# Three PSUM banks for attention scores and one for turned probability blocks, in place of two and two

## The chip, the cores and the metric

The kernel runs on one core of one Trainium2 chip. The metric is the device time of one execution in microseconds (us), lower is better. Times without a unit below are us too.

## The reference, cut to what matters

Two layers over `x` of shape (2, 512, 256). The first is a state-space layer and a mixture of experts; the change doesn't touch it. The second is causal attention with 32 query heads and 8 key/value heads of 64, gated by a small sign network:

```
q, k, v = h @ Wq.T, h @ Wk.T, h @ Wv.T      # 32, 8 and 8 heads of 64; rope on q and k
logits  = where(causal, q @ k.T / 8, min)
attn    = softmax(logits)
out     = (attn @ v) reshaped to (2, 512, 2048) @ Wo.T
x       = x + out * silu(sign_ffn(layernorm(x)))
```

## The kernel before

The program is written engine by engine: TensorE (PE), ScalarE (ACT), VectorE (DVE), GpSimd (POOL) and SyncE (SP, which issues DMAs) each run a list of their own in order, and meet at semaphores. PSUM is cut by hand into 8 banks of 128 x 512 f32, `bank[0]` to `bank[7]`.

Attention runs over 8 groups `g` (one key/value head each). A group has 4 pairs `i` (2 batches times 2 pairs of query heads, `PAIRS`), and each pair is cut into 5 units `k`, so that a unit fills one bank: `SCORES[k]` says which query blocks of 128 rows, with their causal columns, share it. Units are numbered `u = 5 * q + k` with `q = 4 * g + i`; there are 160. Per unit the work is:

- S: PE makes the scores (2 or 4 matmuls of kT, qT, and one that adds the mask) in the unit's score bank; DVE takes the row maxima (L1074, L1070).
- E: ACT takes exp of the score bank into `prob` (L1334), with row sums by the accumulator read behind each.
- N: DVE takes the reciprocal of the sums (L1079) and POOL scales `prob` (L1532), once per head of a pair.
- T: PE transposes four 128 x 128 blocks of `prob` (L1570) into the unit's turned bank. ACT copies that bank, rounded, into `p_hi` (L1341), and then DVE subtracts `p_hi` from the same bank into `p_lo` (L1083).
- A: PE multiplies the values by `p_lo` and `p_hi` (L1908) into banks 4 and 5. After a head's last unit, O on ACT takes it out (L1353) and R on DVE takes the rest (L1092).

Banks 6 and 7 are for making q for the next group (Q, on DVE rope `r`, L1040 and L1041, then `h`, the copy L1308 on ACT) and for the output projection (W, eight matmuls, L1919 to L1922).

The function `schedule(kind)` sorts all of this by step numbers written by hand, for the first group, the middle ones (1 to 6), the last (7, which makes no q) and the tail. In step n come S and E of unit n, T of unit n - 6 (`LAG`) and A of unit n - 8. Every engine takes its operations of a step in the order of their second numbers. Ten steps (half a group) give this list, with Sik for unit k of pair i; the other half is the same with other pairs:

```
step  PE                ACT                DVE
0     S20 T04 A02 W     T04 E20 O00        S20 N T04 W
1     S21 T10 A03 W     T10 E21 Kh         S21 T10 R00 W
2     S22 T11 A04       T11 E22 Vh O01     S22 T11
3     S23 T12 A10 Q     T12 E23 VO         S23 N T12 R01 Vl
4     S24 T13 A11 Q     T13 E24            S24 T13 r
5     S30 T14 A12       T14 E30 O10        S30 N T14 r
6     S31 T20 A13       T20 E31            S31 T20 R10
7     S32 T21 A14       T21 E32 O11        S32 T21
8     S33 T22 A20       T22 E33 h          S33 N T22 R11
9     S34 T23 A21       T23 E34            S34 T23
```

Before, scores alternate between banks 0 and 1, and turned blocks between banks 2 and 3. So S of unit u waits for the exp of unit u - 2, and T of unit u waits for `p_lo` of unit u - 2. The semaphores `exp_done` and `plo_done` start at 2, so that the waits read:

```
pe.wait_ge(exp_done, u + 1)     # S
pe.wait_ge(plo_done, u + 1)     # T
```

Before attention the values of the first batch (`make_v(t)`, t = 0 to 3, six matmuls each, L1574 to L1576) go through banks 0 and 1. Those of the second batch (t = 4 to 7) are made in the first four steps of group 0, between scores, through banks 2 and 3, and ACT copies each out (L1301).

Of the kernel before, what the change touches and what calls it, by code (L numbers as in the profile page):

```python
# [160 lines left out]
PICKED = 2  # L161
CHUNK_AT = [3 + 11.5 * c for c in range(NT)]
Q_MOVES = 4 * 16 * GQ


def q_moved(b, groups):
# [9 lines left out]
def layered_kernel(nc, x, params, consts, select, rope, w_in, w_out, w_moe, w_moe_tail, w_qkv, w_o, w_sign, out):  # L176
# [4 lines left out]
    with ctx:  # L181
# [501 lines left out]
        def _(dve):  # L683
# [376 lines left out]
            def attend(now, steps):  # L1060
                for late, op, i, k in steps:
# [1 line left out]
                    q = g * PAIRS + i  # L1063
                    u = q * 5 + k
                    if op == "S":
                        bk = bank[(i + k) % 2]
                        dve.wait_ge(score_full, u + 1)
                        segs = SCORES[k]
                        if k == 2:
# [7 lines left out]
                    elif op == "N":  # L1077
                        dve.wait_ge(exp_done, q * 5 + (HEADS_AT[k] + 2))
                        vec.reciprocal(rinv[:, i % 2, k, :], rsum[:, i % 2, k, :]).then_inc(rinv_ready, 1)  # L1079
                    elif op == "T":  # L1080
                        b_ = (i + k) % 4
                        dve.wait_ge(phi_done, u + 1)
                        TT(p_lo[:, b_, :], bank[2 + b_ % 2][:, :], p_hi[:, b_, :].bitcast(F32), ALU.subtract).then_inc(plo_done, 1)  # L1083
                    elif op == "R":
                        b, m = i // 2, i % 2
                        dve.wait_ge(ohi_done, 2 * q + k + 1)
                        if q == 0:
                            dve.wait_ge(o_zero, 1)
                        if k == 1 and m == 0 and q > 0:
                            dve.wait_ge(wo_full, g * (BATCH * KC) + 2 * b + 1)  # L1090
                        to = o_rest1[:, m, :] if k else o_rest0[:, b, m, :]
                        STT(out=to, in0=o_hi[:, b, m, :].bitcast(F32), scalar=minus[:, k:k + 1], in1=bank[4 + k][:, :],  # L1092
                            op0=ALU.mult, op1=ALU.add).then_inc(olo_done, 1)
                    elif op == "W":
                        b, m = i // KC, i % KC
                        cs = slice(b * HALF, (b + 1) * HALF)
                        dve.wait_ge(wo_full, g * (BATCH * KC) + (i + 2))
                        if g == 0:
                            vec.tensor_copy(sT[:, m, cs], bank[6 + m][:, :]).then_inc(w_added[m], 1)
                        else:  # L1100
                            TT(sT[:, m, cs], sT[:, m, cs], bank[6 + m][:, :], ALU.add).then_inc(w_added[m], 1)
                    elif op == "M":
                        cs = slice(k * HALF, (k + 1) * HALF)
                        dve.wait_ge(w_added[i], (KVH - 1) * BATCH + (k + 1))
                        dve.wait_ge(g1_ready, KC * (k + 1))
                        TT(sT[:, i, cs], sT[:, i, cs], g1T[:, i, cs], ALU.mult).then_inc(sg_ready, 1)
                    elif op == "X":
                        dve.wait_ge(back_full, i + 1)
                        xt2 = x_tok[:, 2 * i:2 * i + 2, :]
                        TT(xt2, xt2, bank[i][:, :].rearrange("p (t c) -> p t c", c=C), ALU.add).then_inc(x_ready, 1)  # L1110
                    elif op == "r":
                        if now == 0 and i == 1 and k == 0:
                            dve.wait_ge(q_first, 2)
                        rope_q(now * 2 + i, k)
                    elif op == "qa":
                        dve.wait_ge(x_roped[1], now * 2 + i + 1)
                        TT(q_mix[:, :, 0, :], q_mix[:, :, 0, :], q_mix[:, :, 1, :], ALU.add).then_inc(qadd_done, 2)
                    elif op == "ql":
                        dve.wait_ge(qhi_done, now * 2 + i + 1)
                        TT(q_lo[:, :, :], q_mix[:, :, 0, :], q_hi[:, :, :].bitcast(F32), ALU.subtract).then_inc(qlo_done, 2)  # L1120
                    elif op == "Vl":
                        lower_v(now, i)
                    elif op == "Kr":
                        if k == 0:
                            dve.wait_ge(v_out[i], 16)
                            dve.wait_ge(vlo_done, i + 1)
                        rope_k(1, i, k, bank[6 + k])
# [29 lines left out]
        def _(act):  # L1157
# [140 lines left out]

            def copy_v(t):
                act.wait_ge(v_full, t + 1)  # L1300
                actv(v_all[:, t, :], bank[t // TB * 2 + t % 2][:, :], ACT.Copy).then_inc(v_copied, 1)  # L1301

            def upper_q(now, i):
                hh = now * 2 + i
# [16 lines left out]
            def attend(now, steps):  # L1321
                for late, op, i, k in steps:
# [1 line left out]
                    q = g * PAIRS + i  # L1324
                    u = q * 5 + k
                    if op == "E":
                        bk = bank[(i + k) % 2]
                        act.wait_ge(max_ready, u + 1)
                        if k == 0 and (not isinstance(g, int) or q > 1):
                            act.wait_ge(pt_full, q * 5 - 5)  # L1330
# [6 lines left out]
                    elif op == "T":  # L1337
                        b_ = (i + k) % 4
                        act.wait_ge(pt_full, u + 1)
                        act.wait_ge(av_done, u + 1)  # L1340
                        actv(p_hi[:, b_, :], bank[2 + b_ % 2][:, :], ACT.Copy).then_inc(phi_done, 1)  # L1341
                    elif op == "O":
                        b, m = i // 2, i % 2
                        act.wait_ge(av_done, q * 5 + VALUED[k] + 5)
# [223 lines left out]
        def _(pe):  # L1568
# [273 lines left out]
                on_rows(bk[:, :], lambda c: w_h[:, c, k * P:(k + 1) * P], lambda c: w_l[:, c, k * P:(k + 1) * P], b).then_inc(kx_full, 1)  # L1842

            def make_v(t):
                if t % TB > 1:
                    pe.wait_ge(v_copied, t - 1)
                ts = slice(t * P, (t + 1) * P)
                for c in range(KC):
                    ins = split3(bank[t // TB * 2 + t % 2][:, :], xnT_hi[:, c, ts], xnT_lo[:, c, ts], wv0_hi[:, c, :], wv0_lo[:, c, :],
                                 c == 0, c == KC - 1)  # L1850
                ins.then_inc(v_full, 1)

            def attend(now, steps, held):

                for late, op, i, k in steps:
# [7 lines left out]
                    if op == "S":  # L1863
# [3 lines left out]
                            pe.wait_ge(q_in[b], q_moved(b, now + 1))  # L1867
                        if k == 0 and i % 2 == 0:
                            pe.wait_ge(klo_done, now * 2 + (b + 1))
                        pe.wait_ge(exp_done, u + 1)  # L1870
                        for h, j, at in SCORES[k]:
                            n = (j + 1) * P
                            dst = bank[(i + k) % 2][:, at:at + n]
                            qs = qT[:, b, 2 * (i % 2) + h, j * P:(j + 1) * P]
                            mm(dst, qs, kT[:, b, 0, 0:n], start=(h, j, at) == SCORES[k][0], stop=False)  # L1875
                            mm(dst, qs, kT[:, b, 1, 0:n], start=False, stop=False)  # L1876
                        lo, moved = MASKS[k]
                        mm(bank[(i + k) % 2][:, lo:HALF], mask_b[:, :], id_b[:, moved:moved + HALF - lo], start=False,  # L1878
                           stop=True).then_inc(score_full, 1)
                    elif op == "V":  # L1880
                        make_v(i)
                    elif op == "T":
# [2 lines left out]
                            pe.wait_ge(kx_roped, 4)  # L1885
                        if k in (0, 2):
                            pe.wait_ge(prob_ready, q * 2 + (1 if k == 0 else 2))
                        pe.wait_ge(plo_done, u + 1)
                        for h, j, at in TURNED[k]:
                            for r in range(j, TB):  # L1890
                                ins = tr(bank[2 + (i + k) % 2][:, at + (r - j) * P:at + (r - j + 1) * P],
                                         prob[:, i % 2, h, POFF[r] + j * P:POFF[r] + (j + 1) * P])
                        ins.then_inc(pt_full, 1)
                    elif op == "A":
# [173 lines left out]
```

## Time and profile before

| | |
|---|---|
| median of 3 runs | 734.5 us (734.28 to 734.57) |
| the profiled execution | 734.23 us |
| its span, first to last instruction | 732.4 us |
| PE, DVE, ACT, POOL busy over the span | 94%, 70%, 60%, 53% |
| granted TensorE clock over the span | 0.999 of 2.4 GHz |

A profiled execution is one execution. The span leaves 1.8 us of its time outside, before the first instruction and after the last. Busy time is summed over the whole span. An engine's row in a timeline starts when the instruction starts; an "idle before" in brackets names what ended the idle time ahead of it.

### The profile page before, as it was taken

The numbers are of one execution on the slowest core, as the hardware profiler recorded it, in microseconds if no ns is written. First come the engines' busy times: TensorE is split into PE (matmuls) and PEld (weight loads), VectorE is DVE, ScalarE is ACT, GpSimd is POOL, SyncE is SP. The second block draws the span as 40 slices with busy tenths as digits, with TensorE's granted clock in tenths as the row PEclk, the third lists the DMA queues.
The fourth block names the chain that finished last, engine by engine and source line by source line (L and its number), as shares of the span: only waits on it lengthen the run. The fifth ranks groups of instructions, "written<-read, shape, count | busy, mean of one in ns | idle before, by whom it ended". The sixth has DMA issues, their size and how long they took to land.

```text
span 732.4 us, 13492 instructions
## 1 busy us (share of the span) xinstructions
PE 686.1 (94%) x4483; PEld 596.0 (81%) x4483; DVE 513.0 (70%) x1076; ACT 440.7 (60%) x1075; POOL 391.7 (53%) x442
## 2 busy tenths in 40 slices
PE   5999999999999999899889999999999999999995
PEld 3888999989999998687667888888788888787874
DVE  7584656434423335997888878888798878887775
ACT  4446344243331342567678788877877788878772
POOL 1314542423424232137566777877977788777550
PEclk9999999999999999999999999999999999999999
DMA  8158987787877746145442432334323423142011
GB/s 291 53 193 258 289 259 242 244 261 220 266 249 229 222 140 175 34 129 173 128 132 56 119 81 57 96 79 100 78 62 101 95 73 90 49 116 59 1 30 58
DMA packets 108453, 102.25 MB, mean 140 GB/s; under 512 B 51104, under 2 KB 78688, under 8 KB 108256
## 3 DMA queue, kind: packets, MB, share of 16 engines
q1 hardware_dynamic: 106272, 95.62, 45.2%
q0 software_dynamic: 2112, 5.77, 2.5%
q8 instruction: 36, 0.59, 0.3%
q14 instruction: 33, 0.27, 0.1%
HBM read 69.24 MB, written 11.14 MB: 110 GB/s over the span
## 4 chain that ended last, share of the span: by engine, by line
PE 63%; DVE 22%; ACT 7%; issue 5%; POOL 2%; DMA 1%; DVEq 0%; SPq 0%; ACTq 0%; POOLq 0%
PE bank L1735 14%; PE bank L1769 8%; PE bank L1570 6%; PE bank L1908 5%; DVE p_lo L1083 4%; PE bank L1875 3%; DVE nmax L1074 3%; DVE o_rest L1092 3%; PE bank L1574 3%; PE bank L1575 3%; PE bank L1576 3%; PE bank L1876 2%; DVE q_mix L1040 2%; DVE q_mix L1041 2%; ACT prob L1334 2%
## 5 line engine op out<-in xcount | busy, mean ns | idle before, releaser
L1532 POOL TENSOR_TENSOR prob<-prob,rinv 128x128 f32<-128x128 f32 (+3 forms) x256 | 176.4, 721 | 89.8 <-DVE rinv L1079 89.8
L1334 ACT ACTIVATE prob<-bank,nmax 128x512 f32<-128x512 f32 (+3 forms) x256 | 133.1, 525 | 41.1 <-DVE nmax L1074 32.8
L1083 DVE TENSOR_TENSOR p_lo<-bank,p_hi 128x512 fp32r<-128x512 f32 x160 | 109.2, 682 | 56.5 <-ACT p_hi L1341 54.4
L1341 ACT ACTIVATE p_hi<-bank 128x512 fp32r<-128x512 f32 x160 | 95.3, 595 | 42.3 <-PE bank L1570 41.4
L1735 PE MATMUL bank<-xgT,wm 128*128 128x128 f32 x920 | 111.3, 275 | 0.5 <-ACT xgT L1246 0.5
L1735 PEld LDWEIGHTS bank<-xgT,wm 128*128 128x128 f32 x920 | 108.7, 192 | 3.3 <-issue 1.4
L1875 PE MATMUL bank<-kT,qT 128*128 128x512 f32 (+3 forms) x256 | 83.6, 332 | 20.1 <-ACT prob L1334 15.7
L1570 PE MATMUL bank<-cst,prob 128*128 128x128 f32 x640 | 96.6, 274 | 1.4 <-POOL prob L1532 0.7
L1074 DVE TENSOR_REDUCE nmax<-bank 128x1 f32<-128x512 f32 (+2 forms) x192 | 91.0, 500 | 2.1 <-PE bank L1878 2.1
L1908 PE MATMUL bank<-p_lo,v_parts 128*128 128x256 f32 (+3 forms) x288 | 91.7, 341 | 0.2
L1505 POOL DMA_INDIRECT y_rows<-y_row,to_row x21 | 22.7, 1081 | 108.9 <-DVE y_row L943 86.4
L1875 PEld LDWEIGHTS bank<-kT,qT 128*128 128x128 f32 x256 | 48.1, 188 | 35.0 <-ACT prob L1334 27.3
L1570 PEld LDWEIGHTS bank<-cst,prob 128*128 128x128 f32 x640 | 73.1, 141 | 3.3 <-DVE p_lo L1083 0.9
L1876 PE MATMUL bank<-kT,qT 128*128 128x512 f32 (+3 forms) x256 | 74.4, 322 | 0.0
L1908 PE MATMUL bank<-p_hi,v_parts 128*128 128x256 f32 (+3 forms) x288 | 74.2, 304 | 0.0
L1271 ACT ACTIVATE sil<-bank 128x512 f32<-128x512 f32 x23 | 13.7, 596 | 73.4 <-PE bank L1735 54.6
L1769 PE MATMUL bank<-wm,hE 128*128 128x256 f32 x230 | 53.5, 379 | 1.2 <-DVE y_low L948 1.2
L983 DVE TENSOR_TENSOR hE<-sil,bank 128x512 f32<-128x512 f32 x23 | 15.8, 687 | 53.1 <-PE bank L1735 36.0
L1908 PEld LDWEIGHTS bank<-p_lo,v_parts 128*128 128x128 f32 x288 | 52.1, 190 | 0.6 <-issue 0.6
L1908 PEld LDWEIGHTS bank<-p_hi,v_parts 128*128 128x128 f32 x288 | 52.4, 190 | 0.0
L1334 ACT ACTIVATION_READ_ACCUMULATOR prob<-bank,nmax 128x1 f32 x256 | 51.4, 201 | 0.0
L1876 PEld LDWEIGHTS bank<-kT,qT 128*128 128x128 f32 x256 | 48.2, 188 | 2.8
(323 smaller groups left out, 1528.1 us busy)
## 6 DMA issues: line engine op xcount, KB each, us to landing
wm<-in_w_moe SPq DMA_DIRECT2D x23, 1280.0 KB
wm<-in_w_moe SPq DMA_DIRECT2D x23, 640.0 KB
qT<-q_hi SPq DMA_DIRECT2D x124, 64.0 KB, 2.0
qT<-q_lo SPq DMA_DIRECT2D x124, 64.0 KB, 2.0
wo_twice<-wo_hi SPq DMA_DIRECT2D x32, 128.0 KB, 2.5
k_exp<-k_rows SPq DMA_DIRECT2D x56, 64.0 KB, 2.0
wtl<-in_w_moe_tail SPq DMA_DIRECT2D x46, 64.0 KB
y_rows<-gate SPq DMA_DIRECT2D x1, 2048.0 KB, 14.0
```

Source lines behind the costliest of these rows:

```text
L1074: ins = vec.tensor_reduce(out=nmax[:, i % 2, h, j:j + 1], in_=bk[:, at:at + (j + 1) * P], op=ALU.max, axis=AX.X, negate=True)
L1083: TT(p_lo[:, b_, :], bank[2 + b_ % 2][:, :], p_hi[:, b_, :].bitcast(F32), ALU.subtract).then_inc(plo_done, 1)
L1334: ins = actv(prob[:, i % 2, h, POFF[j]:POFF[j] + (j + 1) * P], bk[:, at:at + (j + 1) * P], ACT.Exp, bias=nmax[:, i % 2, h, j:j + 1], accum ...
L1341: actv(p_hi[:, b_, :], bank[2 + b_ % 2][:, :], ACT.Copy).then_inc(phi_done, 1)
L1505: pool.indirect_dma_start(out=y_rows, out_offset=bass.IndirectOffsetOnAxis(ap=to_row[:, n:n + 1], axis=0), in_=y_row[:, n % 2, :], in_offs ...
L1532: ins = GT(seg, seg, rinv[:, i % 2, k, j:j + 1].to_broadcast([P, (j + 1) * P]), ALU.mult)
L1570: return nc.tensor.transpose(dst, src, ident)
L1735: ins = mm(dst, w(c), xgT[:, u, c, :], start=c == 0, stop=c == KC - 1)
L1769: ins = mm(bank[3][:, 0:C], hE[:, u, i * P:(i + 1) * P], wm[:, s, i, PJ:WM] if i < FULL else ptl[:, s, :], start=i == 0, stop=i == HC - 1)
L1875: mm(dst, qs, kT[:, b, 0, 0:n], start=(h, j, at) == SCORES[k][0], stop=False)
L1876: mm(dst, qs, kT[:, b, 1, 0:n], start=False, stop=False)
L1908: ins = mm(bank[4 + h][:, x:y], vs, p[:, b_, at + x - j * P:at + y - j * P], start=first and (h, j) in ((0, 0), (1, 2)), stop=end and (h, ...
```

## The change

The score bank of a unit is now `(5 * q + k) % 3`, so banks 0, 1 and 2 take turns over all units, and S waits for the exp of unit u - 3. Every turned block goes through bank 3, so T waits for `p_lo` of unit u - 1. The second batch's values go through bank 3 alone, each waiting for the copy of the one before. Nothing is added to or taken from the computation, and no engine's order changes.

```diff
+def scores_in(q, k):
+    return (5 * q + k) % 3
+
+
+def values_in(t):
+    return 3 if t >= TB else t % 2
...
-                        bk = bank[(i + k) % 2]
+                        bk = bank[scores_in(q, k)]
...
-                        TT(p_lo[:, b_, :], bank[2 + b_ % 2][:, :], p_hi[:, b_, :].bitcast(F32), ALU.subtract).then_inc(plo_done, 1)
+                        TT(p_lo[:, b_, :], bank[3][:, :], p_hi[:, b_, :].bitcast(F32), ALU.subtract).then_inc(plo_done, 1)
...
-                        actv(p_hi[:, b_, :], bank[2 + b_ % 2][:, :], ACT.Copy).then_inc(phi_done, 1)
+                        actv(p_hi[:, b_, :], bank[3][:, :], ACT.Copy).then_inc(phi_done, 1)
...
             def make_v(t):
-                if t % TB > 1:
+                if t >= TB:
+                    pe.wait_ge(v_copied, t)
+                elif t > 1:
                     pe.wait_ge(v_copied, t - 1)
...
-                        pe.wait_ge(exp_done, u + 1)
+                        pe.wait_ge(exp_done, u)
...
-                            dst = bank[(i + k) % 2][:, at:at + n]
+                            dst = bank[scores_in(q, k)][:, at:at + n]
...
-                        pe.wait_ge(plo_done, u + 1)
+                        pe.wait_ge(plo_done, u + 2)
...
-                                ins = tr(bank[2 + (i + k) % 2][:, at + (r - j) * P:at + (r - j + 1) * P],
+                                ins = tr(bank[3][:, at + (r - j) * P:at + (r - j + 1) * P],
```

## Rows read from the trace of the kernel before

**Rows 1.** Busy time by stretch: us, then busy (and instructions) of PE, PEld, DVE, ACT, POOL.

```profile
448.25:472.00 23.75, 22.77 (x149) 19.52 (x148) 20.07 (x40) 18.82 (x51) 18.67 (x23) 1.00 0.38 96
662.10:684.14 22.04, 20.15 (x136) 17.23 (x135) 17.80 (x36) 17.58 (x50) 14.68 (x20) 1.00 0.20 49
684.14:705.61 21.47, 19.63 (x133) 16.96 (x132) 17.14 (x35) 16.65 (x48) 11.78 (x17) 1.00 0.11 25
705.61:732.40 26.79, 19.32 (x110) 14.87 (x110) 16.34 (x27) 11.07 (x20) 3.80 (x6) 0.97 0.12 40
```

**Rows 2.** Waits, groups 1 to 6 (376.98 to 662.1): us in total, times, longest.

```profile
PEld bank L1875 <- ACT prob L1334: 17.7, 24, 0.9
```

**Rows 3.** Timeline of PE, 448 to 473.5, transposes of steps 2, 3 and 5 to 10: start, us.

```profile
455.10 0.60 PE L1570 MATMUL bank<-cst,prob 128*128 128x128 f32 x4
456.64 0.61 PE L1570 MATMUL bank<-cst,prob 128*128 128x128 f32 x4
...
462.52 0.61 PE L1570 MATMUL bank<-cst,prob 128*128 128x128 f32 x4
...
464.08 0.60 PE L1570 MATMUL bank<-cst,prob 128*128 128x128 f32 x4
...
465.63 0.60 PE L1570 MATMUL bank<-cst,prob 128*128 128x128 f32 x4
...
468.18 0.61 PE L1570 MATMUL bank<-cst,prob 128*128 128x128 f32 x4
...
470.13 0.60 PE L1570 MATMUL bank<-cst,prob 128*128 128x128 f32 x4
...
472.00 0.61 PE L1570 MATMUL bank<-cst,prob 128*128 128x128 f32 x4
```

**Rows 4.** Timelines of ACT and DVE, step 1: the copies of one turned block.

```profile
452.32 0.60 ACT L1341 ACTIVATE p_hi<-bank 128x512 fp32r<-128x512 f32 x1 [0.78 <-PE bank L1570]
...
452.95 0.69 DVE L1083 TENSOR_TENSOR p_lo<-bank,p_hi 128x512 fp32r<-128x512 f32 x1 [0.31 <-ACT p_hi L1341]
```

**Rows 5.** Timelines of DVE, PE and ACT in the tail, round transposes that waited for a bank.

```profile
716.11 0.69 DVE L1083 TENSOR_TENSOR p_lo<-bank,p_hi 128x512 fp32r<-128x512 f32 x1 [1.47 <-ACT p_hi L1341]
...
716.86 0.66 PE L1570 MATMUL bank<-cst,prob 128*128 128x128 f32 x4 [0.52 <-DVE p_lo L1083]
...
717.55 0.60 ACT L1341 ACTIVATE p_hi<-bank 128x512 fp32r<-128x512 f32 x1 [0.32 <-PE bank L1570]
```

**Rows 6.** Timeline of DVE, from one p_lo to the next, steps 3 and 4, then 5 and 6.

```profile
459.04 0.69 DVE L1083 TENSOR_TENSOR p_lo<-bank,p_hi 128x512 fp32r<-128x512 f32 x1 [1.30 <-ACT p_hi L1341]
...
461.44 0.67 DVE L1083 TENSOR_TENSOR p_lo<-bank,p_hi 128x512 fp32r<-128x512 f32 x1
...
463.92 0.65 DVE L1083 TENSOR_TENSOR p_lo<-bank,p_hi 128x512 fp32r<-128x512 f32 x1
...
466.35 0.67 DVE L1083 TENSOR_TENSOR p_lo<-bank,p_hi 128x512 fp32r<-128x512 f32 x1
```

**Rows 7.** Timeline of ACT, from one p_hi to the next, steps 2 and 3, then 8 and 9.

```profile
455.74 0.60 ACT L1341 ACTIVATE p_hi<-bank 128x512 fp32r<-128x512 f32 x1 [1.39 <-PE bank L1570]
...
458.41 0.60 ACT L1341 ACTIVATE p_hi<-bank 128x512 fp32r<-128x512 f32 x1
...
469.98 0.60 ACT L1341 ACTIVATE p_hi<-bank 128x512 fp32r<-128x512 f32 x1
...
472.08 0.60 ACT L1341 ACTIVATE p_hi<-bank 128x512 fp32r<-128x512 f32 x1
```

**Rows 8.** Timelines of group 0: PE and ACT for the values, PE and DVE for transposes.

```profile
328.64 0.53 PE L1574 MATMUL bank<-wv_hi,xnT_lo 128*128 128x512 f32 x1
...
329.83 0.58 ACT L1301 ACTIVATE v_all<-bank 128x512 f32<-128x512 f32 x1
...
348.00 0.60 PE L1570 MATMUL bank<-cst,prob 128*128 128x128 f32 x4
...
350.53 0.65 DVE L1083 TENSOR_TENSOR p_lo<-bank,p_hi 128x512 fp32r<-128x512 f32 x1
```

More of the change, by code:

```diff
@@ L1300, in copy_v @@
                 act.wait_ge(v_full, t + 1)
-                actv(v_all[:, t, :], bank[t // TB * 2 + t % 2][:, :], ACT.Copy).then_inc(v_copied, 1)
+                actv(v_all[:, t, :], bank[values_in(t)][:, :], ACT.Copy).then_inc(v_copied, 1)
             def upper_q(now, i):
@@ L1326, in attend @@
                     if op == "E":
-                        bk = bank[(i + k) % 2]
+                        bk = bank[scores_in(q, k)]
                         act.wait_ge(max_ready, u + 1)
@@ L1848, in make_v @@
                 for c in range(KC):
-                    ins = split3(bank[t // TB * 2 + t % 2][:, :], xnT_hi[:, c, ts], xnT_lo[:, c, ts], wv0_hi[:, c, :], wv0_lo[:, c, :],
+                    ins = split3(bank[values_in(t)][:, :], xnT_hi[:, c, ts], xnT_lo[:, c, ts], wv0_hi[:, c, :], wv0_lo[:, c, :],
                                  c == 0, c == KC - 1)
@@ L1877, in attend @@
                         lo, moved = MASKS[k]
-                        mm(bank[(i + k) % 2][:, lo:HALF], mask_b[:, :], id_b[:, moved:moved + HALF - lo], start=False,
+                        mm(bank[scores_in(q, k)][:, lo:HALF], mask_b[:, :], id_b[:, moved:moved + HALF - lo], start=False,
                            stop=True).then_inc(score_full, 1)
```

## The prediction

> **What bounds the kernel now.** I read four views: busy time by stretch, the waits of the attention stretch, the timelines of PE, ACT and DVE for one half-group, and the tail. In the first the reader should see that attention repeats: ten steps take 23.75 us, PE is busy 22.77 of them at a granted clock of 1.00, which is the 2.4 GHz level, and DVE is busy 20.07 [rows 1]. PE sets the pace and DVE is close behind. In the second, PE's wait in this stretch is one of a kind: score matmuls waiting for the exp that frees their bank, 24 times in 12 half-groups as the weight load sees it, 17.7 us [rows 2]. That is two stalls in a half-group. The third view gives their place. From transpose to transpose the short steps 5 and 6 take 1.56 and 1.55 us, and steps 7, 8 and 9, which hold the same kinds of work, take 2.55, 1.95 and 1.87 [rows 3]. With the start-up of the matmuls behind each, they cost about 6.37 - 3 x 1.56 = 1.7 us in a half-group. This is what the third score bank can give back, and no more.
>
> No row of this stretch has a transpose waiting for its bank: with two banks a block's copies have two steps to finish.
>
> **The scores.** S may now start once the exp of three units back is done. In this order of work the exp of unit u - 3 stands a whole step ahead of the exp that S waits for today, so I take all stalls of S as gone: -1.7 us in each half-group if nothing else waits.
>
> **The turned blocks.** The next transposes may start only after this chain: four transposes, the ACT copy, the DVE subtraction, and then PE. The rows give each link. Transposes 0.60, ACT copy 0.60, DVE 0.69 [rows 3, 4]. Where PE had waited, the transposes took 0.66, ACT started 0.03 behind them, and PE started 0.06 after the end of p_lo (716.80 to 716.86) [rows 5]; DVE started 0.03 after ACT ended [rows 4]. The turnaround is then 0.60 + 0.04 + 0.60 + 0.03 + 0.69 + 0.06 = 2.02 us behind an unhindered transpose, and 2.07 behind one that had waited. No step can be shorter than that, measured from transpose to transpose.
>
> Six of the ten steps are short now: 2, 5, 6, 7, 8 and 9, at 1.54, 1.56, 1.55, 2.55, 1.95 and 1.87, together 11.02 us [rows 3]. The four others have W or Q behind the transposes (23.75 - 11.02 = 12.73 us together) and each is 2.9 us or more, so the chain hides in them. The six become at least 2.02 + 2.02 + 4 x 2.07 = 12.3 us. Two get longer still, because ACT and DVE take their own lists in order:
>
> - Step 6: DVE has both rope products and the maxima of S31 ahead of p_lo. From p_lo to p_lo it needs 2.43 us of work without a gap [rows 6], so the step takes 2.43.
> - Step 9: ACT has E33 and the 1024-wide q_hi copy ahead of p_hi, 2.10 us from p_hi to p_hi without a gap [rows 7]. The step takes 2.10.
>
> The sum is 2.02 + 2.02 + 2.43 + 2.07 + 2.07 + 2.10 = 12.71, against 11.02: +1.69 us in each half-group, with the returned stalls of S already in it. Behind the blocked transpose on PE stand A, Q, W and the next S. That S feeds the maxima and the exp, but they come later in ACT's and DVE's lists than the copies of the same step, so they add nothing of their own. POOL's scaling has about 5 us between its end and the transposes that need it and gets more. Groups 1 to 6 are 12 half-groups: 12 x 1.69 = +20.3.
>
> The last group makes no q, so steps 3 and 4 are short too. Steps 0 and 1 stay at about 6.85 (as 448.25 to 455.10 now). Then 2.02 for step 2; 2.67 for step 3, where ACT has an exp, a copy of values and O ahead [rows 7]; 2.40 for step 4, where DVE has R, the values and the maxima ahead [rows 6]; and five of 2.07: 24.3 us. The two halves take 22.04 and 21.47 now [rows 1], so +2.3 and +2.8, +5.1 in all.
>
> **Group 0.** V60 starts at 328.64 and the copy of the block before it starts only at 329.83 and lasts 0.58 [rows 8]: through one bank V60 starts 1.8 us later, and V70 some 2.6, since the next copy stands behind an exp, q_hi and a value copy. A part is hidden, since the first transposes wait for POOL. Later, transposes start at 348.00 while the p_lo before them starts at 350.53 [rows 8]; they now have to wait until 351.2, 3.2 us. Much of that returns, since DVE and ACT keep their own pace here and S stalls less. Following the three lists through the 20 steps I get between +1.4 (values free) and +4; I take +3.
>
> **The tail.** Five more transposes follow with little between them. Two wait already, one 0.52 us [rows 5]. At 2.07 each the delays add up to 2.0 us at the transposes that start at 716.86 now; behind them stand A and, through DVE, the last subtraction of O, whose wait for DVE's gate products gives back 0.3. I take +1.7, between +1.0 (half of it hidden) and +2.0.
>
> **Sum.** 20.3 + 5.1 + 3.0 + 1.7 = +30.1 against the profiled execution's 734.2 (span 732.4 and 1.8 around it): 764.3. The median of the runs is 0.3 above it, so 764.5.
>
> **Where the skill speaks.** The Trainium skill's "Perfetto Trace Analysis", section "Optimizing Tensor Performance", says that independent matmul groups should rotate through PSUM banks so that ACT and DVE empty one while the next group runs. By that rule alone the scores gain from a third bank and the turned blocks lose their overlap; this trace shows the first as 1.7 us in a half-group and cannot show the second, as it has no case of it outside the tail.
>
> **Rivals.**
> 1. The scores' gain wins and the kernel is faster. The place is the six short steps, and it decides at a turnaround of 11.02 / 6 = 1.84 us. Against it: transposes, copy and subtraction alone are 0.60 + 0.60 + 0.69 = 1.89 with no latency at all. If the turnaround did hide, 12 x 1.7 would come back, and in the last group 43.5 - 2 x (6.85 + 8 x 1.56) = 4.8: 709.
> 2. The bare chain. The extra waits of steps 3, 4, 6 and 9 melt because ACT and DVE regain ground elsewhere, and group 0 costs nothing: 12 x 1.3 + 3.2 (two halves of 6.85 + 2.02 + 7 x 2.07 = 23.4) + 1.7 = +20.5, so 755.
> 3. Queues add up. A late exp or max of a step pushes the next p_hi or p_lo in two or three more of the short steps. If three steps cost 0.3 more each, that is 14 x 0.9 = +12.6: 777.
> 4. PE's clock drops with its new gaps. The granted clock is 0.97 in the tail with PE busy 19.32 of 26.79 us (72%), and 1.00 with 19.63 of 21.47 (91%) [rows 1]; after the change I expect about 22.7 of 25.4 (89%). At 0.97 throughout, PE's 12.7 us of long steps grow by 0.4 each half-group, 14 x 0.4 = +6: 770. The Trainium skill's "TensorE: Matmul & The Clock Gate", section "A second HAM failure mode: psum-queue depth-cycling", tells of a kernel whose short idle times between matmul groups made the clock swing; this trace has such gaps, of up to 1.2 us, at a clock of 1.00, so I give it little.
> 5. The change doesn't do what it says for the scores: the exp three units back is late too, so S still stalls. Its stalls would fall in steps that are now stretched anyway; the time stays near 765.
>
> **How the numbers follow.** Forecast 0.68 (with rival 5), own range 759 to 769; rival 2 0.14; rival 3 0.10; rival 4 0.04; rival 1 0.02; no change 0.02, if single links overlap in a way that I don't see. A change of 0.2% (1.5 us) is about what a measurement of this kernel can tell. The range reaches to rivals 2 and 3 without their far edges, 754 to 775. Faster 0.02, same 0.02, slower 0.96.
>
> **What the profile after would show.** A half-group of 25.4 us where it is 23.75. Waits of score matmuls for exp all but gone. A new row in the waits, transposes (L1570) for p_lo (L1083), about six times in a half-group, mostly 0.4 to 0.6 us. Short steps of 2.07 from transpose to transpose, step 6 near 2.4. PE busy near 90% in attention, the clock at 1.00. In group 0, V matmuls that wait for ACT's copy, up to 1.8 us. Wrong would be: fewer waits of transposes than six, a turnaround under 1.9, or long steps (W, Q) that get longer too.

## The result and the profile after

The changed kernel takes 770.1 us (768.24 to 770.8, median of 4 runs) against 734.5 in the same measurement: a ratio of 1.048 (1.0466 to 1.0491), 35.6 us slower. The forecast was 764.5, with a range of 754 to 775. The profiled execution is the longest of the four: 770.8, span 769.0. In what follows line numbers of the changed kernel are 8 higher than before from the maxima on (the transposes are L1578, `p_hi` L1349, `p_lo` L1091) and 10 higher from the score matmuls on (the first is L1885), and vary by a few in the experiments.

First comes busy time by stretch, the answer to [rows 1]. The columns are us, then busy (and instructions) of PE, PEld, DVE, ACT, POOL, then the granted clock. The five rows are group 0, one half-group, the two halves of the last group, and the tail.

```profile
325.34:382.60 57.26, 49.26 (x275) 40.54 (x273) 46.69 (x82) 39.92 (x102) 34.72 (x39) 0.94 0.52 147
408.36:434.11 25.75, 23.33 (x147) 19.76 (x147) 20.36 (x40) 19.01 (x51) 18.64 (x23) 1.00 0.35 88
691.77:716.30 24.53, 20.97 (x135) 17.59 (x135) 17.98 (x36) 17.54 (x49) 13.90 (x19) 1.00 0.18 44
716.30:740.82 24.52, 20.33 (x132) 17.25 (x132) 17.93 (x35) 17.57 (x49) 12.44 (x17) 1.00 0.09 22
740.82:769.00 28.18, 19.06 (x109) 14.54 (x110) 14.76 (x23) 10.14 (x17) 2.76 (x4) 0.97 0.11 38
```

A half-group takes 25.75 us where it took 23.75. PE is busy 91% of it where it was 96%, and every other engine's share fell as well.

The waits over groups 1 to 6 (total, times, longest) show what PE waits for now. The row of [rows 2], scores waiting for exp, is gone. In its place transposes wait 72 times for `p_lo`, six times in each half-group:

```profile
PE bank L1578 <- DVE p_lo L1091: 29.6, 72, 0.6
PEld bank L1578 <- DVE p_lo L1091: 22.4, 36, 0.9
```

PE's timeline from step 2 on, transposes alone, the rows that answer to [rows 3]:

```profile
415.25 0.60 PE L1578 MATMUL bank<-cst,prob 128*128 128x128 f32 x4
417.36 0.63 PE L1578 MATMUL bank<-cst,prob 128*128 128x128 f32 x4 [0.40 <-DVE p_lo L1091]
420.32 0.60 PE L1578 MATMUL bank<-cst,prob 128*128 128x128 f32 x4
423.25 0.61 PE L1578 MATMUL bank<-cst,prob 128*128 128x128 f32 x4
425.37 0.63 PE L1578 MATMUL bank<-cst,prob 128*128 128x128 f32 x4 [0.39 <-DVE p_lo L1091]
427.73 0.66 PE L1578 MATMUL bank<-cst,prob 128*128 128x128 f32 x4 [0.62 <-DVE p_lo L1091]
429.90 0.63 PE L1578 MATMUL bank<-cst,prob 128*128 128x128 f32 x4 [0.37 <-DVE p_lo L1091]
432.01 0.66 PE L1578 MATMUL bank<-cst,prob 128*128 128x128 f32 x4 [0.34 <-DVE p_lo L1091]
434.11 0.66 PE L1578 MATMUL bank<-cst,prob 128*128 128x128 f32 x4 [0.31 <-DVE p_lo L1091]
```

The six short steps take 2.11, 2.12, 2.36, 2.17, 2.11 and 2.10: 12.97 us. The four long ones take 12.78, with the first two from 408.36 on.

DVE's timeline has the end of the chain for two of these steps, 5 and 7:

```profile
424.53 0.69 DVE L1091 TENSOR_TENSOR p_lo<-bank,p_hi 128x512 fp32r<-128x512 f32 x1 [0.30 <-ACT p_hi L1349]
...
429.06 0.69 DVE L1091 TENSOR_TENSOR p_lo<-bank,p_hi 128x512 fp32r<-128x512 f32 x1
```

These subtractions end at 425.22 and 429.75. PE starts at 425.37 and 429.90, 0.15 behind each; the chain of the forecast had 0.06.

ACT's timeline has a list that the forecast didn't count. Between the `p_hi` of T21 and that of T22 stand two exps and O, and from one `p_hi` to the next it needs 2.20 us with hardly a gap:

```profile
428.43 0.60 ACT L1349 ACTIVATE p_hi<-bank 128x512 fp32r<-128x512 f32 x1 [0.29 <-PE bank L1578]
428.96 0.47 ACT L1342 ACTIVATE prob<-bank,nmax 128x256 f32<-128x256 f32 x1
...
429.43 0.47 ACT L1342 ACTIVATE prob<-bank,nmax 128x256 f32<-128x256 f32 x1
...
430.01 0.59 ACT L1361 ACTIVATE o_hi<-bank 64x512 fp32r<-64x512 f32 x1
430.63 0.60 ACT L1349 ACTIVATE p_hi<-bank 128x512 fp32r<-128x512 f32 x1
```

In group 0 PE waits nine times, three times for the copy of a V and six times for `p_lo`. The longest wait of a V for the copy of the one before, and the two longest of a transpose:

```profile
331.70 0.50 PE L1582 MATMUL bank<-wv_hi,xnT_lo 128*128 128x512 f32 x1 [0.99 <-ACT v_all L1309]
...
354.45 1.09 PE L1578 MATMUL bank<-cst,prob 128*128 128x128 f32 x4 [2.44 <-DVE p_lo L1091]
...
374.41 1.02 PE L1578 MATMUL bank<-cst,prob 128*128 128x128 f32 x4 [1.68 <-DVE p_lo L1091]
```

Four transposes take 1.09 and 1.02 there, and 0.66 after the shorter waits. The granted clock (third column from the right) in stretches of 2 us around these two places is the reason:

```profile
352.00:354.00 2.00, 0.02 (x1) 0.00 (x0) 2.00 (x4) 0.32 (x1) 0.19 (x1) 1.00 0.85 150
354.00:356.00 2.00, 1.55 (x8) 1.58 (x9) 0.97 (x3) 2.00 (x5) 2.00 (x4) 0.52 0.92 288
356.00:358.00 2.00, 2.00 (x8) 1.62 (x8) 1.35 (x2) 1.79 (x6) 0.70 (x2) 0.63 0.37 97
374.00:376.00 2.00, 1.59 (x8) 1.59 (x8) 1.62 (x3) 2.00 (x6) 1.45 (x2) 0.64 0.00 0
376.00:378.00 2.00, 2.00 (x10) 1.48 (x9) 1.05 (x2) 2.00 (x7) 0.00 (x0) 0.51 0.66 236
```

After PE had stood still from 352 to 354 the clock was at its lower level (1.2 GHz) for most of the next 4 us, and again behind the wait that ends at 374.41. The four runs show it too: the one with a mean granted clock of 0.999 took 768.24, the profiled one with 0.992 took 770.8. About 1.9 us of the median's 35.6 are then this clock, by 770.1 - 768.24 (an estimate from one run).

Where the 36.6 us of span went, stretch by stretch (after less before, cut at the same transposes; those of before start at 376.98, 662.01 and 705.61, so the cut at 662.10 in [rows 1] is 0.09 late):

| stretch | after - before | forecast |
|---|---|---|
| ahead of attention, which the change doesn't touch | +1.2 | 0 |
| group 0: 57.26 - 52.88 | +4.4 | +3.0 |
| groups 1 to 6: 309.17 - 285.03 | +24.1 | +20.3 |
| last group: 49.05 - 43.60 | +5.45 | +5.1 |
| tail: 28.18 - 26.79 | +1.4 | +1.7 |

The first row is the clock too. The code there is the same, and PE has the same wait of 1.62 us in both traces (before the transposes at 304.48 and 304.82). The clock behind it is 1.00 in the kernel before and 0.57 in the changed one:

```profile
306.00:308.00 2.00, 1.42 (x11) 1.09 (x9) 2.00 (x5) 1.84 (x5) 0.00 (x0) 1.00 0.00 0
```

```profile
306.00:308.00 2.00, 1.98 (x9) 1.66 (x10) 1.93 (x6) 1.36 (x4) 0.00 (x0) 0.57 0.00 0
```

Of the twelve experiments below, two have this in their trace and start attention at 325.27 and 325.45; the ten others start it between 324.20 and 324.37. So the 1.2 us belong to the profiled execution and not to the change.

### The profile page after: what moved, and what is told of

Its sections match the earlier page's. It is cut to its first block, busy times and chain, and to the rows that moved or that the text cites. A ratio compares the mean times of both kernels' runs of the same rounds, so it can differ in the third digit from the quotient of the medians.

```text
span 769.0 us, 13490 instructions
## 1 busy us (share of the span) xinstructions
PE 698.8 (91%) x4481; PEld 603.9 (79%) x4483; DVE 519.5 (68%) x1076; ACT 444.4 (58%) x1075; POOL 392.5 (51%) x442
## 4 chain that ended last, share of the span: by engine, by line
PE 68%; ACT 13%; DVE 12%; issue 5%; DMA 1%; POOL 0%; SPq 0%; DVEq 0%; ACTq 0%
PE bank L1743 14%; PE bank L1578 10%; PE bank L1777 8%; ACT p_hi L1349 5%; DVE p_lo L1091 5%; PE bank L1582 5%; PE bank L1584 4%; PE bank L1583 4%; PE bank L1918 4%; ACT prob L1342 3%; PE bank L1886 2%; PE bank L1932 2%; PE bank L1930 2%; PE bank L1929 2%; PE bank L1931 2%
## 5 line engine op out<-in xcount | busy, mean ns | idle before, releaser
L1091 DVE TENSOR_TENSOR p_lo<-bank,p_hi 128x512 fp32r<-128x512 f32 x160 | 110.3, 689 | 69.3 <-ACT p_hi L1349 66.3
L1349 ACT ACTIVATE p_hi<-bank 128x512 fp32r<-128x512 f32 x160 | 95.7, 598 | 95.5 <-PE bank L1578 94.5
L1578 PE MATMUL bank<-cst,prob 128*128 128x128 f32 x640 | 101.2, 281 | 45.6 <-DVE p_lo L1091 45.6
L1578 PEld LDWEIGHTS bank<-cst,prob 128*128 128x128 f32 x640 | 70.3, 142 | 62.6 <-DVE p_lo L1091 36.5
L1885 PE MATMUL bank<-kT,qT 128*128 128x512 f32 (+3 forms) x256 | 80.7, 321 | 0.0
L1886 PE MATMUL bank<-kT,qT 128*128 128x512 f32 (+3 forms) x256 | 74.7, 323 | 0.0
L1885 PEld LDWEIGHTS bank<-kT,qT 128*128 128x128 f32 x256 | 48.4, 189 | 3.5
```

What stands on the lines that cost most here:

```text
L1091: TT(p_lo[:, b_, :], bank[3][:, :], p_hi[:, b_, :].bitcast(F32), ALU.subtract).then_inc(plo_done, 1)
L1349: actv(p_hi[:, b_, :], bank[3][:, :], ACT.Copy).then_inc(phi_done, 1)
L1578: return nc.tensor.transpose(dst, src, ident)
```

## The experiments

Medians below are in us; each run had its own measurement of the kernel before, which lay between 734.5 and 734.7.

**Scores on two banks again, turned blocks on one.** This takes the third score bank away and leaves the rest.

```diff
-    return (5 * q + k) % 3
+    return (5 * q + k) % 2
...
-                        pe.wait_ge(exp_done, u)
+                        pe.wait_ge(exp_done, u + 1)
```

> The changed kernel with its scores back on two banks (unit number modulo 2, S waits for the exp of two units back); turned blocks and values stay on one bank. My theory: from transpose to transpose the steps are now set by the copies of the one turned bank (2.1 us), so the exp of two units back is done before S is reached and the third score bank is worth nothing here: 770 us, within 2 of the changed kernel. Rival: the third score bank does give its 1.7 us back in each half-group, and the chain costs 3.4: then 770 + 12 x 1.7 + 4 = 794 us.

Measured: 769.6 (768.18 to 770.95), ratio 1.047 (1.0455 to 1.0492). A half-group takes 25.76 us, with the same ten steps to 0.02. So the third bank for scores is worth nothing in this kernel once the turned blocks have one bank.

**The chain ends at `p_hi`, first attempt.** The subtraction reads a constant in SBUF in place of the bank, so that the kernel leaves out the low part of the turned blocks, and the next transposes wait for `p_hi` only.

```diff
-                        pe.wait_ge(plo_done, u + 2)
+                        if u > 0:
+                            pe.wait_ge(phi_done, u)
...
-                        TT(p_lo[:, b_, :], bank[3][:, :], p_hi[:, b_, :].bitcast(F32), ALU.subtract).then_inc(plo_done, 1)
+                        TT(p_lo[:, b_, :], turns[:, 0, :], p_hi[:, b_, :].bitcast(F32), ALU.subtract).then_inc(plo_done, 1)
```

> The changed kernel, but DVE's subtraction for p_lo reads an SBUF tile of the same size in place of the turned bank (so the low part of the turned blocks is left out of the result), and the next transposes wait for ACT's copy alone. The chain from transposes to transposes is then 0.66 + 0.03 + 0.60 + 0.06 = 1.35 us, under the 1.56 us of a short step. My theory: no transpose waits, and the third score bank shows what it is worth: 12 half-groups near 22.1 us, 709 to 718 us in all. Rival: something else of the change (scores going round three banks, the values) makes the kernel slow: it stays above 755 us.

Measured: 766.86 (765.33 to 766.93), ratio 1.043 (1.0412 to 1.0447). The number lies where the rival had it, but this is no test of either, because the experiment changed a duration. In the groups of instructions (busy, mean ns, idle before) of this kernel:

```profile
L1540 POOL TENSOR_TENSOR prob<-prob,rinv 128x128 f32<-128x128 f32 (+3 forms) x256 | 213.9, 864 | 74.7 <-DVE rinv L1087 74.7
L1091 DVE TENSOR_TENSOR p_lo<-turns,p_hi 128x512 fp32r<-128x512 f32 x160 | 161.2, 1007 | 33.4 <-ACT p_hi L1349 32.3
```

In the changed kernel the two have means of 721 and 689 ns. With both operands in SBUF the subtraction takes 1.01 us in the mean, and POOL's scaling is slower too. Transposes now wait for `p_hi` (26.4 us in 36 waits between 396 and 652), which stands behind exps that wait for DVE.

**The chain ends at `p_hi`, with the subtraction's cost kept.** The subtraction reads bank 2, which nothing writes in attention (so the low part is left out here too), and scores keep to banks 0 and 1.

```diff
-    return (5 * q + k) % 3
+    return (5 * q + k) % 2
...
-                        TT(p_lo[:, b_, :], bank[3][:, :], p_hi[:, b_, :].bitcast(F32), ALU.subtract).then_inc(plo_done, 1)
+                        TT(p_lo[:, b_, :], bank[2][:, :], p_hi[:, b_, :].bitcast(F32), ALU.subtract).then_inc(plo_done, 1)
```

> Scores alternate between two banks again, all turned blocks still go through bank 3, but the next transposes wait for ACT's copy p_hi alone and no longer for the subtraction: the subtraction reads bank 2, which nothing writes in attention, in place of bank 3 (so the low part p_lo is left out of the result; its duration, its operands' places and its order stay those of the kernel before). The chain becomes 0.60 (transposes) + 0.04 + 0.60 (copy) + 0.06 = 1.30 us, less than the shortest step (1.55). Theory (the subtraction at the end of the chain is what cost the time): a half-group falls from 25.75 back to 23.8 to 24.0 (step 9 may keep 2.10 in place of 1.87, because ACT needs that from copy to copy), group 0 costs 0 to 2, the tail under 1: 735 to 740 us. Rival (having one bank at all, or something else in the changed program, costs the time): half-groups stay over 25.3, 763 us or more.

Measured: 747.2 (747.2 to 747.62), ratio 1.017 (1.0156 to 1.019). Neither number came. The half-group is 24.52 us, and PE's timeline has this in it:

```profile
421.82 0.66 PE L1578 MATMUL bank<-cst,prob 128*128 128x128 f32 x4
...
423.62 0.50 PE L1885 MATMUL bank<-kT,qT 128*128 128x512 f32 x1 [0.60 <-ACT prob L1342]
...
426.72 0.66 PE L1578 MATMUL bank<-cst,prob 128*128 128x128 f32 x4 [0.32 <-ACT p_hi L1349]
...
428.82 0.66 PE L1578 MATMUL bank<-cst,prob 128*128 128x128 f32 x4 [0.32 <-ACT p_hi L1349]
```

Scores wait for exp as before the change, and two transposes wait for a `p_hi` that has an exp and O, or an exp and q_hi, ahead of it in ACT's list. I had summed the chain alone (1.30) and left ACT's list out. The first experiment, at 25.76, has the same banks as this one and the wait for `p_lo`. So it is the subtraction at the end of the chain that costs 25.76 - 24.52 = 1.24 of the 2.0 us in a half-group, and the theory holds for this part. What is left against the kernel before, 24.52 - 23.75 = 0.77, comes with the one bank and the wait for `p_hi`; two of its steps, 8 and 9, are set by waits for `p_hi`, and no run takes it apart further.

**Order of the two waits.** A transpose of k = 0 or 2 waits for POOL's scaling and for `p_lo`. These are the steps whose turnaround was 0.09 longer.

```diff
+                        pe.wait_ge(plo_done, u + 2)
                         if k in (0, 2):
                             pe.wait_ge(prob_ready, q * 2 + (1 if k == 0 else 2))
-                        pe.wait_ge(plo_done, u + 2)
```

> The changed kernel with the two waits of a transposes group in the other order: first p_lo of the block before, then POOL's scaling. After the change transposes of units k = 0 and 2, which have both waits, start 0.15 us behind the end of p_lo, those with one wait 0.05 to 0.06. My theory: the second wait in the program is a separate instruction on PE's queue and costs 0.09 us behind the release; in the other order it is over when p_lo comes, or the other way round: 3 such steps in a half-group, 14 x 3 x 0.09 = 3.8 us less, 766 us. Rival: the 0.1 us belongs to the weight load of these transposes, not to the waits: no change, 770 us.

Measured: 767.4 (767.3 to 767.61), ratio 1.0444 (1.0426 to 1.0461). PE's timeline from step 5 to step 8, transposes alone:

```profile
420.69 0.61 PE L1578 MATMUL bank<-cst,prob 128*128 128x128 f32 x4
422.71 0.66 PE L1578 MATMUL bank<-cst,prob 128*128 128x128 f32 x4 [0.30 <-DVE p_lo L1091]
425.17 0.66 PE L1578 MATMUL bank<-cst,prob 128*128 128x128 f32 x4 [0.69 <-DVE p_lo L1091]
427.24 0.65 PE L1578 MATMUL bank<-cst,prob 128*128 128x128 f32 x4 [0.30 <-DVE p_lo L1091]
```

Steps 2, 5 and 7 fall to the 2.02, 2.02 and 2.07 of the forecast, so the 0.09 is real and comes from having the `p_lo` wait last. But steps 6 and 8 grow by 0.10 and 0.09, and the half-group ends at 25.71: 0.04 better. Steps 5 and 6 together take 4.48 in both kernels, and 7 and 8 together 4.28 and 4.27. The first pair is set by DVE's list, 2.47 from `p_lo` to `p_lo`, the second by ACT's, 2.20 from `p_hi` to `p_hi`; a late start inside a pair costs nothing. Most of the rest of this run's gain is the clock: in its trace attention starts 1.0 us earlier than in the changed kernel's, at 324.37, and group 0 takes 55.75 for 57.26. The wait of 2.36 us there is followed by transposes of 0.66, not 1.09.

**The sum of q in group 0 later on DVE.** In group 0 DVE itself adds q, ahead of a `p_lo` that a transpose waits 2.44 us for.

```diff
-        return z + [(n + 2, 8.1, "qa", i, 0), (n + 3, 4.5, "h", i, 0), (n + (5 if i == 2 else 4), 8.3 if i == 2 else 3.3, "ql", i, 0)]
+        return z + [(n + 3, 3.1, "qa", i, 0), (n + 3, 4.5, "h", i, 0), (n + (5 if i == 2 else 4), 8.3 if i == 2 else 3.3, "ql", i, 0)]
```

> The changed kernel with one operation moved in the first group: DVE's addition of the two rope products (1.2 to 2.0 us) stands behind the maxima and the p_lo of the next step in place of ahead of them, twice. My theory: PE's two long waits of group 0 (2.44 and 1.68 us for p_lo) shrink to under 1 us, the granted clock no longer falls behind them, and the time drops by 3 to 5 us to 766 us, with a clock of 0.999. Rival: the wait goes elsewhere (the q copy on ACT comes later and the exps behind it), the clock still falls, 770 us.

Measured: 768.91 (768.62 to 770.25), ratio 1.047 (1.0453 to 1.0488). The wait of 2.44 became two of 0.75 and 1.12, and a new wait of 2.59 appeared at 374.86, with slow transposes (1.06 us at 376.17) behind it. The wait moved; the run does not separate the theories.

**The second batch's values alone.** The kernel before, with only V through bank 3.

```diff
-                actv(v_all[:, t, :], bank[t // TB * 2 + t % 2][:, :], ACT.Copy).then_inc(v_copied, 1)
+                actv(v_all[:, t, :], bank[3 if t >= TB else t % 2][:, :], ACT.Copy).then_inc(v_copied, 1)
...
-                if t % TB > 1:
+                if t >= TB:
+                    pe.wait_ge(v_copied, t)
+                elif t > 1:
                     pe.wait_ge(v_copied, t - 1)
...
```

> The kernel before with one part of the change: the second batch's values go through bank 3 alone, each waiting for the copy of the one before; scores and turned blocks keep two banks each. Theory (the forecast's first term of group 0): V60 and V70 start 0.3 to 2.6 us later, most of it hidden because the first transposes wait for POOL; +0.3 to +2.0, 735 to 736.5 us. Rival (all hidden): within 0.2 of the kernel before. Rival (they are the larger part of group 0's +4.4): 738 us or more.

Measured: 736.53 (735.73 to 737.55), ratio 1.0025 (1.0016 to 1.0035): +1.9, at the top of what was expected. Part of it is the clock: five of the ten executions have a granted clock of 0.998 or more and take 735.73 to 736.05, the five others 0.996 or 0.997 and 737.01 to 737.55. In the trace group 0 takes 54.22 for 52.88, so the values alone cost 1.3. V60 starts at 330.59 for 328.64 [rows 8], and the first transposes start 1.5 later.

**The change from group 1 on.** Group 0 keeps the banks of before; the banks change hands at its end.

```diff
+def scores_in(q, k):
+    u = 5 * q + k
+    return (u + 1) % 3 if u >= STEPS else (q + k) % 2
+
+def turned_in(q, k):
+    return 3 if 5 * q + k >= STEPS - LAG else 2 + (q + k) % 2
...
```

> One part of the change undone: in group 0 the scores, the turned blocks and the second batch's values keep the banks of the kernel before; from group 1 on there are three score banks and one turned bank, as in the changed kernel. Theory (group 0 costs +4.4 by the two traces, the clock that falls behind its two waits of 2.4 and 1.7 us included): the changed kernel's 770.1 less 4.4, 765 to 766.5 us, the transposes of group 0 at 0.66 or less and the half-groups still 25.75. Rival (the loss of group 0 is only pushed behind its end, since the first of the later groups would have taken the delay anyway): 768 or more.

Measured: 766.09 (765.84 to 766.17), ratio 1.0425 (1.0408 to 1.0442), clock 0.999, half-groups 25.77. As expected: group 0 with its clock costs 4.0 of the 35.6, and that is its own. Against the one run of the changed kernel at the same clock, 768.24, it is 2.15.

**A third score bank that takes nothing from the turned blocks.** From group 1 on, scores use banks 0, 1 and 7, turned blocks keep 2 and 3, and q and W are made in bank 6 alone (the first half of q one step earlier). The second kernel is its control: the same serial bank 6, scores on 0 and 1.

```diff
+def scores_in(q, k):
+    u = 5 * q + k
+    if u < STEPS:
+        return (q + k) % 2
+    return u % 3 if u % 3 < 2 else 7
+
+def made_in(now, k):
+    return 6 if 0 < now < KVH else 6 + k
...
-        z = [(n, 8, "Q", i, 0), (n + 1, 8, "Q", i, 1), (n + 1, 8, "r", i, 0), (n + 2, 8, "r", i, 1), (n + 3, 6, "a", i, 0),
+        z = [(n - 1, 8, "Q", i, 0), (n + 1, 8, "Q", i, 1), (n - 1, 8, "r", i, 0), (n + 2, 8, "r", i, 1), (n + 3, 6, "a", i, 0),
...
-                        pe.wait_ge(exp_done, u + 1)
+                        pe.wait_ge(exp_done, u if u >= STEPS else u + 1)
...
```

> A version in which scores get the third bank without taking it from the turned blocks: from group 1 on, scores use banks 0, 1 and 7 in turn (S waits for the exp of three units back), turned blocks keep banks 2 and 3, and the output projection and q are made in bank 6 alone (the first half of q one step earlier, its rope behind the maxima of that same step). Group 0 and the tail as before. Theory (the stalls of S cost 1.7 us in a half-group and a third bank removes them all): a half-group of 22.1 to 22.7 in place of 23.75 (12 of them: -13 to -20), the last group's halves near 20.3 in place of 22.04 and 21.47 (-2 to -3): 712 to 720 us. Rival A (DVE, busy 20.07 of 23.75, or POOL's scaling takes over as the next wait, or bank 6 alone makes new waits): 723 to 733. Rival B (the stalls have another cause than the bank, exp is late anyway): within 2 us of the control with the same serial bank 6, whatever that takes.

> Control for the five-bank version: output projection and q through bank 6 alone and the first half of q a step earlier, but scores on banks 0 and 1 as before, bank 7 idle from group 1 to the last. Both theories: about the kernel before, 733 to 739 us (a W of the second bank that waits for DVE costs 0 to 0.3 in a half-group; the moved q may shift stalls of S by a few tenths either way). If it is far from 734.5, the five-bank version must be read against this one.

Measured: five banks 733.99 (733.13 to 736.1), ratio 0.9997 (0.9986 to 1.0008); control 736.35 (736.26 to 737.73), ratio 1.0028 (1.0016 to 1.0039). The theory of the stalls falls. In the mean of groups 1 to 6 the control's half-group is 23.90, the five banks' 23.65: 0.25 us, where I had taken up to 1.7. The medians are 2.4 apart; the fastest executions, all at a clock of 0.998 or more, are 3.1 apart (736.26 and 733.13), about 12 x 0.25. PE, DVE and ACT at the end of a half-group of the five-bank kernel:

```profile
421.69 0.60 PE L1581 MATMUL bank<-cst,prob 128*128 128x128 f32 x4
...
424.02 0.66 PE L1581 MATMUL bank<-cst,prob 128*128 128x128 f32 x4 [0.61 <-DVE p_lo L1094]
```

```profile
421.46 0.68 DVE L1085 TENSOR_REDUCE nmax<-bank 128x1 f32<-128x512 f32 x1
...
423.27 0.69 DVE L1094 TENSOR_TENSOR p_lo<-bank,p_hi 128x512 fp32r<-128x512 f32 x1 [1.05 <-ACT p_hi L1352]
```

```profile
420.98 0.48 ACT L1345 ACTIVATE prob<-bank,nmax 128x256 f32<-128x256 f32 x1 [0.35 <-DVE nmax L1081]
...
421.44 0.47 ACT L1345 ACTIVATE prob<-bank,nmax 128x256 f32<-128x256 f32 x1
...
422.02 0.59 ACT L1364 ACTIVATE o_hi<-bank 64x512 fp32r<-64x512 f32 x1
422.64 0.60 ACT L1352 ACTIVATE p_hi<-bank 128x512 fp32r<-128x512 f32 x1
```

In groups 1 to 6 no score waits any more, but PE, now ahead, waits for a turned bank although there are two: `p_lo` at 423.27 waits for `p_hi` at 422.64, behind O and an exp, and that exp for maxima at the end of a DVE list without a gap from 417.15 to 422.2. Step 7 falls from the control's 2.47 us to 1.64, and steps 9 and 0 take 2.33 and 3.81 for 1.86 and 3.43. I read it so: the stall of [rows 2] was where the pace of the DVE and ACT lists showed, not what set it.

**PE's long steps cut in two.** Each W and each q of groups 1 to 7 is issued as two halves in neighbouring steps, with the ropes and the copies of q later, once on each kernel.

```diff
-            own += [(10 * b + 9 + LAG + TO_V + 3 + m, 8.5, "W", b * KC + m, 0)]
+            n = 10 * b + 9 + LAG + TO_V + 3 + 2 * m
+            own += [(n - 1, 8.5, "w", b * KC + m, 0), (n, 8.5, "W", b * KC + m, 0)]
...
-        z = [(n, 8, "Q", i, 0), (n + 1, 8, "Q", i, 1), (n + 1, 8, "r", i, 0), (n + 2, 8, "r", i, 1), (n + 3, 6, "a", i, 0),
-             (n + 4, 6, "a", i, 1), (n + 5, 8, "h", i, 0)]
+        z = [(n - 1, 8, "q", i, 0), (n, 8, "Q", i, 0), (n + 1, 8, "q", i, 1), (n + 2, 8, "Q", i, 1), (n + 1, 8, "r", i, 0),
+             (n + 3, 8, "r", i, 1), (n + 4, 6, "a", i, 0), (n + 5, 6, "a", i, 1), (n + 6, 8, "h", i, 0)]
```

> The kernel before (two and two banks) with PE's long steps cut in two: each output projection and each q of groups 1 to 7 is issued as two halves in neighbouring steps (4 and 3 matmuls), so that PE's steps are 1.55 to 3.2 us in place of 1.55 to 3.4; q's ropes, sums and copy come a step later. Theory (DVE's and ACT's lists of steps 4 to 9, which have no gap, are what the stalls of S come from, and an even PE feeds them evenly): a half-group of 22.9 to 23.6, 723 to 733 us. Rival (their lists set the pace wherever PE's long work stands, or q a step later makes new waits): 734 us or more.

> The same cut of PE's long steps on the changed kernel (three score banks, one turned bank). Theory (the loss is only in steps shorter than the 2.07 us chain, and W and Q cover it where they stand): steps 9, 0 and 1 take 2.5, step 2 about 3.2, steps 3 to 5 about 2.25, steps 6 to 8 2.07 to 2.4: a half-group of 23.8 to 24.3 in place of 25.75 and 745 to 753 us, so most of the loss comes back with the single bank kept. Rival (the single turned bank costs by more than the chain against the short steps, every step pays something): 25.2 or more, 762 us or more.

Measured: on the kernel before 746.48 (746.39 to 747.9), ratio 1.016 (1.0142 to 1.0176); on the changed one 761.11 (761.04 to 764.35), ratio 1.037 (1.0349 to 1.0397). Half of the expectation holds: on the changed kernel steps 3 and 4 take 2.26 us with no wait. The half-groups are 25.24 and 25.49 in turn all the same, 25.35 in the mean. In the kernel before it is 24.72: scores wait 1.31 us for an exp, and W's first half, a step earlier, waits 0.84 for DVE's R.

**Only q cut, W as it was,** on the changed kernel. The edit is that of the lines of q above; both halves of W stand in their old step, one behind the other.

> The changed kernel (three score banks, one turned bank) with only q cut: the two products of q of groups 1 to 6 are issued as four halves of 3 matmuls behind the transposes of steps 2, 3, 4 and 5, in place of whole ones in steps 3 and 4; ropes in steps 4 and 6, copy q_hi in step 9; the output projection stays where it was. The earlier cut kernel took 2.26 us for steps with a half q and lost at W, which waited for DVE's R. Theory (a step costs the larger of PE's own work in it and the chain of 2.1 us, so covered steps cost nothing): steps 0 and 1 6.85, steps 2 to 5 4 x 2.26 = 9.04, steps 6 to 9 2.1, 2.43, 2.2 and 2.1: 24.6 to 24.9 us for a half-group in place of 25.75, 756 to 761 us. Rival (the delays of DVE's and ACT's lists come on top wherever PE's work stands): 25.4 or more, 765 us or more.

Measured: 780.99 (779.42 to 781.02), ratio 1.062 (1.0606 to 1.0641), slower than any other. The half-group is 26.68. DVE's timeline shows why:

```profile
426.73 0.69 DVE L1092 TENSOR_TENSOR p_lo<-bank,p_hi 128x512 fp32r<-128x512 f32 x1 [0.57 <-ACT p_hi L1350]
427.33 0.74 DVE L1101 SCALAR_TENSOR_TENSOR o_rest<-o_hi,minus,bank 128x512 fp32r<-128x512 f32 x1
427.99 0.68 DVE L1049 TENSOR_TENSOR q_mix<-bank,turns 128x512 f32<-128x512 f32 x1
428.59 0.68 DVE L1050 TENSOR_TENSOR q_mix<-bank,turns 128x512 f32<-128x512 f32 x1
429.19 0.68 DVE L1079 TENSOR_REDUCE nmax<-bank 128x2 f32<-128x512 f32 x1
429.79 0.68 DVE L1092 TENSOR_TENSOR p_lo<-bank,p_hi 128x512 fp32r<-128x512 f32 x1
```

The late rope landed in the step that has R already. From `p_lo` to `p_lo` DVE has 3.06 us of work without a gap, and PE's step takes 3.14. Step 4, in which PE has only half of a q left, has R, the values and the maxima on DVE ahead of its `p_lo` and takes 2.96. My sum had PE's work and the bare chain in it and not DVE's list: the same kind of omission as in the second attempt at `p_hi`, where ACT's was missing.

## Why the prediction was right, and where its sizes were off

- **The mechanism.** "The next transposes may start only after this chain" is shown. The waits are the six per half-group that the prediction named. Five of its six short steps grew, step 7 came down from 2.55 to 2.17 as the sum had it, and its long steps hardly moved (12.78 for 12.73). Ending the chain at `p_hi` gives 22.9 of the 35.6 us back.
- **The turnaround and a missing list.** Forecast 12.71 for the six short steps, measured 12.97. The term that was too small is that of steps 7 and 8, 2 x 2.07 = 4.14 for 4.28. The forecast had the bare chain there and left out ACT's list between two copies (two exps and O, 2.20 us), and it had DVE's list in step 6 a little short (2.43 for 2.47, which makes steps 5 and 6 4.48 for 4.45). In step 2 PE starts 0.15, not 0.06, behind `p_lo`, +0.09. Steps 5 and 7 have this late start too, but the kernel with the waits' order turned shows that it costs nothing there. With 0.05 of the long steps this is 0.14 + 0.03 + 0.09 + 0.05 = 0.31 in a half-group, 12 x 0.31 = 3.7 of the 5.6 us between 764.5 and 770.1. The other 1.9 is about what the clock took: the run at 0.999 stands at 768.24.
- **The lists.** Step 9 at 2.10 and the two pairs 5, 6 and 7, 8 show that DVE's and ACT's lists between two copies are a floor beside the chain. The prediction used this for steps 6 and 9. Where I left it out, at step 8 and in the expectations for the cut kernels and for `p_hi`, the numbers missed.
- **The scores.** "This is what the third score bank can give back, and no more" was right as a bound and no use as a price. With the turned blocks on one bank it gave 0, with two it gave 0.25 us in a half-group. The forecast's sum doesn't rest on it, as the chain was the larger in each short step. Rival 1's 709 does. The five-bank kernel, in which turned blocks keep their two banks, stands at 734.0, so that time looks out of reach even with a hidden turnaround.
- **Group 0.** Forecast +3.0 (1.4 to 4), measured +4.4 in the profiled execution and 4.0 by leaving the change out of it. The kernel with the waits' order turned has long waits of the same size (2.36 and 1.69) at a clock of 1.00, and its group 0 takes 55.75 - 52.88 = +2.9. So the waits cost what was forecast, and the other 1.5 is the clock, for which the forecast had no term. The values are 1.3 of the 2.9, V60 starting late as forecast. Rival 4 had the clock fall for the small gaps of every half-group; those ran at 1.00. The Trainium skill's "TensorE: Matmul & The Clock Gate", section "A second HAM failure mode: psum-queue depth-cycling", which the prediction weighed there, tells of short gaps between groups of matmuls; with 72 gaps of up to 0.6 us in groups 1 to 6 no such swing is in this trace. That rival 4's time, 770, is the measured one is chance.
- **The last group and the tail.** 24.53 and 24.52 a half for 24.3; +1.4 for +1.7. No step of the last group is off by more than 0.1 us.
- **What stays open.** The likeliest case's own range ended at 769, 1.1 short of the median. Why the clock falls in some executions and not in others, behind the same wait, no run here shows. Nor does one take apart the 0.77 us that are left in a half-group when the chain ends at `p_hi`.

## What to carry to other kernels

Before taking a second buffer away, write down for each step of the schedule the largest of four numbers: the producer's own work, the turnaround of one buffer with its latencies, and for each consumer its whole list from one emptying to the next. A consumer's list can span two steps, as ACT's did over steps 7 and 8. The sum of the maxima is then an estimate of the new time (here 25.6 us for a half-group of 25.75), and moving work off the longest engine helps only as far as the next of the four. A stall that ends at a buffer's release is not yet worth its length: give the buffer from an idle place first and see whether the wait moves, as it did here (1.7 us of stalls, 0.25 us gained).

## What the runs showed of the hardware that I had not expected

- The same pair of semaphore waits costs PE 0.15 us from the last release to the start with the late one second (425.22 to 425.37), and 0.06 with the late one first (422.65 to 422.71 in the kernel with the order turned). Turning the order won 0.04 us in a half-group.
- A DVE subtraction of 128 x 512 took 689 ns in the mean with one operand in PSUM. With both in SBUF it took 1007 ns (655 at least, 1743 at most), while POOL's scaling went from 721 to 864 ns.
- The granted clock fell behind PE waits of 2.44 and 1.68 us in the changed kernel and not behind waits of 2.36 and 1.69 in the kernel with the waits' order turned (transposes at 353.34 and 371.95 of 0.66 us). Ahead of attention it fell behind a wait of 1.62 us in one execution and not behind the same wait in another. So the length of the wait alone doesn't decide it.
